# A decoder block's self attention: the order of VectorE's and TensorE's work, and one subtraction moved to GpSimd

## The reference, cut to what matters

```python
def _sparse_mask(seq_len):
    idx = jnp.arange(seq_len)
    block_id = idx // BLOCK_SIZE                      # blocks of 64
    local = block_id[:, None] == block_id[None, :]
    gp = np.linspace(0, seq_len - 1, 8).astype(np.int64)
    is_global = jnp.zeros((seq_len,), dtype=bool).at[gp].set(True)
    return local | is_global[:, None] | is_global[None, :]

xn = _layernorm(x)
q, k, v = (split_heads(xn @ W + b) for W, b in ((Wq, bq), (Wk, bk), (Wv, bv)))   # 16 heads of 8
scores = jnp.einsum('bhqd,bhkd->bhqk', q, k) / sqrt(8)
scores = jnp.where(mask, scores, -inf)
attn = jax.nn.softmax(scores, axis=-1)
x = x + (merge_heads(jnp.einsum('bhqk,bhkd->bhqd', attn, v)) @ Wo + bo)
```

## Time and profile before

| | us |
|---|---|
| median of 3 runs | 580.83 (580.59 to 580.95) |
| the profiled execution | 579.96 |
| its span in the trace | 577.8 |
| TensorE matmul busy | 481.1 (83%) |
| VectorE busy | 420.3 (73%) |
| ScalarE busy | 297.2 (51%) |
| GpSimd busy | 293.1 (51%) |

### The profile page before, as it was taken

The page is one execution under the profiler, slowest core; times in us unless marked ns, Lnnn a source line. Parts: engine busy times, 40 slices in busy tenths (PEclk is TensorE's granted clock), DMA queues, the critical chain, the costliest instruction groups (busy, mean ns, idle before and its releaser), DMA issues. The chain is left out here.

```text
span 577.8 us, 16568 instructions
## 1 busy us (share of the span) xinstructions
PE 481.1 (83%) x5675; PEld 363.3 (63%) x5675; DVE 420.3 (73%) x1308; ACT 297.2 (51%) x756; POOL 293.1 (51%) x540
## 2 busy tenths in 40 slices
PE   1968988888888888859999999999777999999700
PEld 1856666666666666546767677676645788888600
DVE  7658989999788888867999899888572444344237
ACT  2636566555555566524665646565432544444337
POOL 4743444433333333210357878777772477777720
PEclk9979999999999999987999999999989999999765
DMA  6526444455354465415233333332024333333149
GB/s 190 110 56 124 66 65 61 81 115 112 100 107 100 103 107 101 102 41 142 62 82 83 96 91 79 93 81 80 32 77 130 101 116 115 114 114 93 56 159 301
DMA packets 96002, 58.30 MB, mean 101 GB/s; under 512 B 24560, under 2 KB 92224, under 8 KB 95920
## 3 DMA queue, kind: packets, MB, share of 16 engines
q1 hardware_dynamic: 74016, 39.80, 29.6%
q10 hardware_dynamic: 17328, 7.54, 6.3%
q0 software_dynamic: 4576, 9.91, 5.1%
HBM read 20.83 MB, written 17.50 MB: 66 GB/s over the span
## 5 line engine op out<-in xcount | busy, mean ns | idle before, releaser
L730 DVE TENSOR_REDUCE nmax<-ps 128x8 f32<-128x512 f32 x128 | 85.3, 682 | 19.1 <-PE ps L1559 15.2
L627 POOL DMA_INDIRECT expert_out<-ey,xt x79 | 75.9, 961 | 41.0 <-DVE ey L1121 20.8
L485 POOL TENSOR_SCALAR veps<-mv 128x2 f32<-128x2 f32 x48 | 11.4, 237 | 163.5 <-issue 117.8
L1252 ACT ACTIVATE probs<-ps 128x512 f32<-128x512 f32 x128 | 73.5, 602 | 7.9 <-PE ps L1764 5.7
L574 POOL DMA_INDIRECT expert_in<-xn,sloti x64 | 65.6, 1025 | 17.6 <-issue 17.6
L1116 DVE TENSOR_TENSOR eh<-ps,sg 128x256 f32<-128x256 f32 x40 | 17.0, 425 | 56.4 <-ACT sg L1450 56.4
L1962 PE MATMUL ps<-wgu,turned 128*128 x160 | 41.3, 380 | 0.3 <-ACT turned L1444 0.3
L1559 PE MATMUL ps<-kbd,qs 96*64 96x128 bf16 x512 | 38.0, 293 | 2.4 <-DMA kbd<-part 1.9
L487 POOL TENSOR_TENSOR rstd<-veps,minus_half 128x2 f32<-128x2 f32 x48 | 36.7, 764 | 4.0
L1444 ACT COPY turned<-ps 128x512 f32<-128x512 f32 (+1 forms) x43 | 23.8, 555 | 25.2 <-PE ps L1955 22.0
L671 DVE TENSOR_SCALAR xn<-x_rows,mv,rstd 128x128 f32<-128x128 f32 x64 | 24.9, 429 | 15.1 <-POOL rstd L487 14.9
(11 more groups left out here) (242 smaller groups left out, 1346.9 us busy)
## 6 DMA issues: line engine op xcount, KB each, us to landing
qs<-part ACTq DMA_DIRECT2D x96, 64.0 KB
kbd<-part SPq DMA_DIRECT2D x192, 32.0 KB
xt<-expert_in SPq DMA_DIRECT2D x80, 72.0 KB
ck_scr<-wgu SPq DMA_DIRECT2D x6, 512.0 KB, 3.6
qs<-part SPq DMA_DIRECT2D x48, 64.0 KB
ckbd<-ck_scr SPq DMA_DIRECT2D x16, 192.0 KB, 2.9
kbd<-part SPq DMA_DIRECT2D x48, 64.0 KB
wgu<-in_L_ffn_gate_up_w SPq DMA_DIRECT2D x4, 512.0 KB, 3.8
```

The source lines that it names most:

```text
L627: pool.indirect_dma_start(ys, bass.IndirectOffsetOnAxis(xt[p][:, E:E + 1].bitcast(I32), 0), ey[q % 4][:, j, :], None).then_inc(e_(f"out{q ...
L730: v.tensor_reduce(nmax[:, u, 8 * half:8 * half + 8], bank[:, :].rearrange("p (h k) -> p h k", k=64), AX.X, ALU.max, negate=True).then_inc( ...
L1252: a_.activation(probs[:, 2 * i:2 * i + 2, :], P2[i % 2][:, :].rearrange("p (j q) -> p j q", j=2), ACT.Exp, scale=SCALE).then_inc(s("probs" ...
```

## The change

VectorE adds the global rows (`global_rows`) before it takes the maximum over the global queries, not after. After the four row maxima it goes on with the whole maximum and the shift at once; the maskings `self_vg` and, except in the last body, `global_heads_out` come behind the shift. The residual of batch b+2 is made on GpSimd, at the end of its body b; those of batches 0 and 1 stay on VectorE, before the loop. TensorE turns the next batch's shift after both products of `global_values_out` and not between them.

```diff
@@ GpSimd, self_body
+                if has(b + 2):
+                    self_rest(b + 2, p)
+
+            def self_rest(b, p):
+
+                pool.wait_ge(s_("part"), 3 * b + 1)
+                at_least(pool, s_("part"), 3 * b)
+                g.tensor_tensor(res[:, :], qk[p][:, :], part[:, 0, :], ALU.subtract).then_inc(s_("res"), 1)
@@ VectorE, self_body
                 if has(b - 1):
                     attended(b - 1)
+                    global_rows(b - 1)
                 if b == 0:
                     self_last_part(1)
                 if has(b):
                     global_query_max(b)
-                if has(b - 1):
-                    global_rows(b - 1)
...
                 self_maxima(b + 1, 0, 0)
                 self_maxima(b + 1, 0, 1)
-                if has(b + 2):
-                    self_rest(b + 2, p)
-                elif CROSS and b + 2 == B:
+                if CROSS and b + 2 == B:
                     cross_rest(0)
-                if has(b):
+                if b + 1 == B:
                     global_heads_out(b)
                 self_maxima(b + 1, 1, 0)
                 self_maxima(b + 1, 1, 1)
                 if has(b + 1):
-                    self_vg(b + 1, 1 - p)
                     whole_max(b + 1)
                     shift_rows(s_, b + 1, 1 - p)
+                    self_vg(b + 1, 1 - p)
+                    if has(b):
+                        global_heads_out(b)
@@ TensorE, global_values_out
                 mm(OD[:, 0:S], vg[p][:, 0, :], probs_g[:, :], start=False, stop=True, skip_group_check=True)
+                mm(OD[:, S:2 * S], vg[p][:, 1, :], probs_g[:, :], start=False, stop=True, skip_group_check=True).then_inc(s_("od"), 1)
                 if has(b + 1):
                     turn_shift(s_, b + 1)
-                mm(OD[:, S:2 * S], vg[p][:, 1, :], probs_g[:, :], start=False, stop=True, skip_group_check=True).then_inc(s_("od"), 1)
```

## The result

The changed kernel takes 584.50 us in the median of 12 runs (581.82 to 588.71), the kernel before 580.46 in 12 runs beside it: 1.008 times before, 95% interval 1.0055 to 1.0106. It is slower, as forecast, but by more than twice the forecast's 1.8 us. The profiled execution took 584.0 us, 4.0 over the profiled execution of before, with a span of 582.2 us, 4.4 over its span.

The account below looks back on a forecast made before the run. The loop closing over TensorE and VectorE through `x_new` was taken to bound the kernel. Ten bodies of 0.16 (1.6), -0.3 for the residual and 0.5 in body 14 gave +1.8 on 580.83: 582.6 us, range 579.6 to 585.0.

Parts of the forecast that it names:

- the closed loop: Self attention body: `x_new`, TensorE's projections and scores, VectorE's maxima, shift, spread and attended rows bound it; body 0.16 us longer.
- a wait of 0.2 to 0.3 us of the reciprocal in each body: Sign expected in the changed profile: VectorE's reciprocal waits this long for ScalarE's exponential sum, ahead of `x_rows`.
- ten bodies of 0.16: Self attention loop: of 14 periods, ten show the body's 0.16 us lengthening, 1.6 us in all.
- four times 0.16: Four of the 14 loop periods, where TensorE waits for regrouped keys up to 0.7 us, absorb the 0.16.
- -0.3 for the residual: Loop bodies where VectorE's residual took up to 0.95 us: its removal gives up to 0.26 more, -0.3 us overall.
- The last body's +0.5: Body 14: cross attention's residual stays on VectorE and masks move before the spread, 0.3 + 0.2 = 0.5 us longer.
- Transfers hiding the loss: Rival, chance 0.26: keys arrive just in time in most bodies, hiding the longer loop; only 0.5 us remains, 581.3.
- TensorE taking its waits back: Rival, chance 0.16: the reciprocal does not hold VectorE up; projections 0.38 us earlier in ten bodies, -3.8 us, 577.0.
- GpSimd blocking VectorE: Rival, chance 0.08: GpSimd's later head copies clash with VectorE's loop steps, 0.27 us per body, 3.8 us more, 586.4.
- a shift step over 0.2 us: Sign that would prove the forecast wrong: VectorE's shift steps in the changed profile longer than 0.2 us.
- GpSimd's residual: End of GpSimd's body: residual takes 1.22 us, between 0.61 and 1.91, ending before ScalarE needs it, so costs nothing.

Follow-up runs that it names:

- e4: Changed kernel with VectorE's reciprocal of the global queries' sum behind `x_rows` instead of ahead of it: ratio 1.0067 to before, median 582.59 us.
- e14: Kernel before with three matmuls that nobody reads in each TensorE wait for `rden` in the last two cross attention bodies: ratio 1.0027, slower chip.
- e15: Kernel before, unaltered, traced on a slower chip beside its own copy: ratio 1.0024.
- e13: Changed kernel with three matmuls that nobody reads in each TensorE wait for `rden` in the last two cross attention bodies: ratio 1.0070, slower chip.
- e17: Same kernel as e13, run again beside the unfilled changed kernel on one slower chip: 625.72 us, ratio 1.0075 to before.
- e10: Changed kernel, unaltered, measured again with a second trace: median 585.55 us, ratio 1.0099 to before.
- e16: Changed kernel, unaltered, traced on a slower chip: 628.74 us, ratio 1.0126 to before.
- e3: Changed kernel with the residual on VectorE again, GpSimd without it: ratio 1.0105 to before, median 585.76 us.
- e6: Changed kernel with both masks ahead of the third maximum and the reciprocal behind `x_rows`: ratio 1.0008 to before, median 580.45 us.

## Why the prediction was right on the sign and wrong on the size

*Held: the closed loop.* The forecast placed the steps of a body, counted from the first scores, at 2.85 us (third maximum), 4.17 (whole maximum), 5.11 (third part), 5.82 (spread), 9.49 (rows), 11.26 (reciprocal), 11.39 (`x_rows`) and 11.97 (projections). Body 6 has 2.86, 4.25, 5.22, 5.92, 9.59, 11.38, 11.46 and 12.03. The wait of TensorE for `x_rows`, the smaller wait for the shift and VectorE's wait of 0.51 us ahead of the third maximum are there. e4 shows that the reciprocal is the link.

One sign of the forecast did not come: a wait of 0.2 to 0.3 us of the reciprocal in each body. It is counted twice in the steady part, and in body 6 it is 0.10; what the reciprocal costs `x_rows` is the 0.25 between 11.46 and e4's 11.21.

*The failed step, mis-sized: "ten bodies of 0.16".* That it shows in ten bodies was right. The four periods that ended in a wait for keys before are, taken together, as long in the changed kernel; the other ten are 2.6 us longer, 0.26 each instead of 0.16 (one is 0.02 shorter, one 0.80 longer). The size was read from one body. In body 6 the period is 0.22 longer: between the end of the maxima and the whole maximum 0.10 us went by (129.68 to 129.78), where I had taken 0.04 from another pair of steps, and 0.97 from there to the third part instead of 0.94; all that follows is about 0.1 later. And body 8 of before, with `x_rows` at 11.23, isn't its shortest: three bodies have it at 11.07 to 11.12, while none of the changed kernel has it under 11.46. Over the 14 bodies `x_rows` comes 4.0 us later (the starts behind the first scores add up to 164.7 instead of 160.6 us), 0.29 each. From `x_rows` to the next scores 1.4 us come back (26.0 instead of 27.4), since of the four waits for keys one is left, 0.6 us instead of 1.9; the forecast had 0.64 for this, four times 0.16. The remainder is the 2.6 us from the first scores of batch 1 to those of batch 15 (188.0 to 190.7). The mean of three traces of before (first, e14, e15) and five of the changed kernel says the same: 4.0 us later, 2.1 back. "-0.3 for the residual" isn't to be seen: the two bodies where it took 0.90 and 0.95 us became 0.09 and 0.21 longer all the same. The last body's +0.5 came out as it was in the traces at full clock: 20.2 to 20.7 us. Together the loop lost 3.1 us against 1.8 forecast, in five traces of the changed order 211.3 to 211.9, in four of before's 208.1 to 208.8.

*The failed step, missing: a term for TensorE's clock.* The forecast treated all behind the loop as unchanged, which put this term at nothing without a reason. In both traces on the faster chips it lost 2.7 us in two bodies, at 1.2 GHz right after TensorE's waits for `rden` and `attT`. How often it falls there is a matter of the execution: of the 15 traces (after's and before's first among them) without fill nine have one or two such stretches, of the five with fill none. Only e13 and e17 of these five have an unfilled kernel beside them that fell in most of its traces (two, two and no stretches). Each stretch costs 1.1 to 1.6 us on the faster chips (13.0, 14.2 and 15.7 us with none, one and two). Over all runs the mean granted clock of the changed kernel was 0.9485 and 0.9519 (e10) where before has 0.954, and among the runs of one kernel 0.01 of clock goes with 3 us (a straight line through the runs of each kernel on the faster chips). By this, an estimate, some 0.5 to 1.6 us of the 4.0 and 5.3 go with the clock. That the changed kernel's runs meet the falls more often is what these means and e17's 3.0 us speak for, but the one trace each on the slower chip goes the other way, and why it should is not settled.

*What stays open.* The start was 2.2 us shorter in the first pair of traces and 0.6 to 2.7 in pairs of other groups; no experiment took it apart. In the mean of three traces of before (first, e14, e15) and the five of the changed kernel the loop is some 3 us longer and the start 1.5 shorter, which leaves about 1.4. That this lies near the forecast's 1.8 is luck: its loss was too small, and it did not have the gain of the start. With the clock's share it is 1.9 to 3.0 us. The runs were 4.0, 5.3 and 6.7 us longer (first, e10, e16), so 1 to 5 us have no stage that these traces show.

*The rivals.* Transfers hiding the loss (581.3): true for 1.4 of the 4.0 us by which `x_rows` came later, and so for the four bodies that the forecast gave them, but not for the other ten. TensorE taking its waits back (577.0): wrong, the reciprocal did hold `x_rows` up; and with it out of the way (e4) the loop only came level with before's, not 3.8 us below: `x_rows` then starts as the statistics ahead of it on VectorE end (136.31 us in e4's trace, the aggregation at 136.03), not behind its product. GpSimd blocking VectorE (586.4): near the measured time but for another reason. The head copies run beside the whole maximum in all 14 bodies of after, and in five of them it took 0.23 to 0.36 us instead of 0.19, 0.4 us more in all. In body 8:

```profile
157.33 0.28 DVE L801 TENSOR_TENSOR nmax<-nmax,nmaxg 128x32 f32<-128x32 f32 x1
```
```profile
156.82 0.76 POOL L522 TENSOR_TENSOR kg<-qk,constants 128x16 f32<-128x16 f32 x3
```

In body 6 it took 0.19 beside the same copies (129.78), so this is not 0.27 in each body; by its sign (a shift step over 0.2 us) the forecast had this rival alive in those five. In e3, where GpSimd has no residual and its copies end earlier, it took 0.19 in all 14. The Trainium skill (SBUF — State Buffer, Who interferes with whom) names such a pair, two inputs in SBUF on VectorE beside a GpSimd instruction that reads there; the trace agrees in five bodies and shows nothing in nine.

*GpSimd's residual* took 1.157 us, near the forecast's 1.22, which was a guess between two bounds; it ended 0.2 us or more before ScalarE took it up (170.79 and 170.99 us at the closest), and ScalarE's idle time ahead of it is the 2.0 us of its own issues, as before. The Trainium skill (GPSIMD Engine Reference, 3.1 Elementwise) states about 2.6 cycles for an element, which at 1.2 GHz is 1.11 us for 512 elements, an estimate from that page; the trace is 0.05 us above it.

## What to carry to other kernels

Follow the loop that closes over all engines, and put small work into the wait at which that loop stands still anyway: the same two masks cost 2.2 us more of the 14 periods in one place (e4) than in the other (e6), and a reciprocal that waits for another engine belongs behind the step that this loop needs. Read the size of an effect from all bodies and not from one: the body that was read gave 0.16 where the mean of ten was 0.26. Compare kernels by the place of a step in an undisturbed body, which repeats to 0.01 us, before sums over a stage, which differ by 2 us between traces of one kernel. And where a change moves the time by more than its own stage shows, compare the stages one by one with the granted clock beside them: in two of the three traces of the changed kernel without fill two bodies far behind the change lost nearly as much as the loop.

## What the runs showed of the hardware

TensorE went to 1.2 GHz in a dense stage after waits no longer than 0.83 us, in some executions and not in others of the same kernel; in the last self attention body it did so after a wait of 1.25 us (e13), and not after one of 1.24 (first trace of after). In the five traces with three matmuls of 128x512 in each wait for `rden` there was no such stretch in those two bodies; two of the five (e13, e17) are of a kernel that had them in two of three traces without the matmuls. Chips differ: before takes 579.3 to 580.6 us on three and 621.5 to 622.0 on two others. The self attention loop is as long on both kinds within 0.6 us; 39 us of the difference lie behind the cross attention stage (158.0 us there in the first trace, 197.4 in e15).
